# A long convolution, linear attention and two mixtures of experts: mixtures re-ordered, attention's front one batch further ahead

## What is computed

```python
x = x + conv(_layernorm(x))        # long convolution, by DFT
x = x + moe(_layernorm(x))         # mixture of experts
x = x + attention(_layernorm(x))   # causal linear attention, 16 heads of 8
x = x + moe(_layernorm(x))         # the same weights again

def attention(x):                  # q, k, v = split(x @ w_attn)
    q, k = elu(q) + 1, elu(k) + 1
    y[t] = (q[t] . sum_{s<=t} k[s] v[s]^T) / (q[t] . sum_{s<=t} k[s] + 1e-6)
    return y @ w_proj

def moe(x):                        # top-1 of 8 experts, and a shared expert
    logits = x @ gate_w; e = argmax(logits); score = sigmoid(max(logits))
    xs = x * score
    routed = (silu(xs @ rt_gate[e]) * (xs @ rt_up[e])) @ rt_down[e]
    shared = (silu(x @ sh_gate) * (x @ sh_up)) @ sh_down
    return shared + routed
```

## Time and profile before

| | |
|---|---|
| median of 3 runs | 617.75 us (612.2 to 619.62) |
| the profiled execution | 617.06 us |
| its span, first to last instruction | 614.2 us |
| mean granted TensorE clock | 0.924 of full |
| busy in the span: PE, PE weight load | 499.2 us (81%), 384.7 us (63%) |
| busy: DVE, ACT, POOL | 382.8, 249.9, 363.2 us |

### The profile page before, as it was taken

How to read it: one execution, slowest core, us unless ns; L and a number is a source line. 1 busy time by engine, 2 the same in 40 slices (tenths; PEclk the granted TensorE clock), 3 DMA queues, 4 the chain that set the end, 5 groups by cost and what they waited for, 6 DMA issues and landing times.

```text
span 614.2 us, 13049 instructions
## 1 busy us (share of the span) xinstructions
PE 499.2 (81%) x3876; PEld 384.7 (63%) x3876; DVE 382.8 (62%) x1191; ACT 249.9 (41%) x639; POOL 363.2 (59%) x490
## 2 busy tenths in 40 slices
PE   2456999986899799994878878888877999899960
PEld 0244787775666599973555655565646665699950
DVE  3645899877765666633566576666556676666633
ACT  2123353422345255542454545454543444255530
POOL 4022665734887156664777787878594886066650
PEclk9968999997999999997788899898986899999995
DMA  8999999900111123315000000000000111133319
GB/s 245 346 199 193 190 190 185 143 1 1 36 48 40 44 81 89 96 53 138 1 3 1 1 3 2 1 3 2 2 2 17 37 43 45 34 85 93 84 53 268
DMA packets 52384, 47.49 MB, mean 77 GB/s; under 512 B 4154, under 2 KB 48891, under 8 KB 52190
## 3 DMA queue, kind: packets, MB, share of 16 engines
q1 hardware_dynamic: 47184, 35.84, 27.3%
q0 software_dynamic: 4544, 9.35, 4.5%
q10 hardware_dynamic: 590, 1.50, 0.8%
HBM read 17.79 MB, written 28.87 MB: 76 GB/s over the span
## 4 chain that ended last, share of the span: by engine, by line
PE 53%; DVE 17%; POOL 11%; issue 10%; ACT 4%; DMA 2%; SPq 1%; DVEq 0%; POOLq 0%; ACTq 0%
PE bank L731 50%; POOL prod L705 4%; DVE residual L1386 2%; POOL step_rstd L258 2%; DVE prod L1329 2%; POOL normed L691 1%; POOL normed L687 1%; ACT silu_sh L1073 1%; PE bank L805 1%; DVE conv_xv L1470 1%; DMA rows<-routed 1%; DVE stats L246 1%; PE bank L741 1%; DVE conv_xv L1238 1%; DVE scores_odd L1543 1%
## 5 line engine op out<-in xcount | busy, mean ns | idle before, releaser
L624 POOL DMA_INDIRECT routed<-row_out,row_token x78 | 75.1, 963 | 72.9 <-DVE row_token L1367 68.7
L731 PE MATMUL bank<-row_in_t,row_weights 128*128 128x128 f32 x624 | 83.8, 277 | 2.8 <-DVE row_weights L1359 1.5
L731 PEld LDWEIGHTS bank<-row_in_t,row_weights 128*128 128x128 f32 x624 | 75.7, 191 | 4.3 <-ACT row_in_t L1052 2.8
L612 POOL DMA_INDIRECT sorted_rows<-rows,place x64 | 62.8, 982 | 20.5 <-issue 13.7
L731 PE MATMUL bank<-prod,silu_sh 32*128 32x512 f32 x256 | 41.1, 715 | 27.8 <-POOL prod L705 27.8
L1052 ACT ACTIVATE wide<-bank 128x512 f32<-128x512 f32 x56 | 30.8, 597 | 79.3 <-PE bank L741 57.8
L731 PE MATMUL bank<-wide,weights_sb 128*128 128x512 f32 x128 | 58.9, 603 | 0.4 <-ACT row_out L1052 0.4
L705 POOL TENSOR_SCALAR prod<-silu_sh,tables_sb 128x256 f32<-128x256 f32 x64 | 36.4, 585 | 25.2 <-DVE silu_sh L1529 25.2
L731 PE MATMUL bank<-experts,row_act 128*128 x312 | 50.2, 283 | 1.4 <-ACT row_out L1052 0.8
L1359 DVE TENSOR_SCALAR row_weights<-experts 128x512 f32 x78 | 33.6, 430 | 27.1 <-issue 24.4
L1092 ACT ACTIVATE row_silu<-bank 128x256 f32<-128x256 f32 x78 | 30.0, 384 | 48.5 <-PE bank L731 47.9
(11 more groups left out here) (176 smaller groups left out, 1135.2 us busy)
## 6 DMA issues: line engine op xcount, KB each, us to landing
sorted_rows<-zeros SPq DMA_DIRECT2D x1, 17028.0 KB, 98.8
row_in<-sorted_rows SPq DMA_DIRECT2D x78, 64.5 KB, 1.8
rows<-routed SPq DMA_DIRECT2D x16, 256.0 KB, 4.5
out<-residual SPq DMA_DIRECT2D x8, 256.0 KB, 4.0
tables_sb<-tables SPq DMA_DIRECT2D x1, 1536.0 KB, 16.7
routed<-row_out,row_token POOLq DMA_INDIRECT x78, 2.4
experts<-rt_gate SPq DMA_DIRECT2D x1, 1024.0 KB, 10.2
experts<-rt_up SPq DMA_DIRECT2D x1, 1024.0 KB, 12.8
```

The source lines that it names most:

```text
L612: pool.indirect_dma_start(sorted_rows, bass.IndirectOffsetOnAxis(ap=place[:, t:t + 1].bitcast(U32), axis=0), rows[:, t, :], None).then_inc ...
L624: pool.indirect_dma_start(routed, bass.IndirectOffsetOnAxis(ap=row_token[:, r:r + 1].bitcast(U32), axis=0), row_out[:, r, :], None).then_i ...
L731: return pe.matmul(out_, lhsT, rhs, start=start, stop=stop, **kw)
```

## The change

- **Mixtures, order.** In each step PE's `turn` goes behind `up` and `rank`, ACT's `keep` behind the Silus. The first steps that stood whole beside the last steps of the layer before are taken apart into `turn`, `gate`, `rank`, `up_half`, `choose`, `find_place`, `apply_kept` and so on, each placed by itself. The first pair's shared `up` and Silu move there too.
- **Tile table.** `tile_table` is split; its first part (experts) goes ahead of that step's gate-up, the second behind it, `blank_table` into the row tiles' start. Three weight buffers instead of two, the first three filled ahead.
- **Late shared pair.** In both layers, in halves: `up` of the first half stands ahead of the last two row-downs.
- **Final loads.** `routed` is laid out so that a partition's 32 tokens follow each other; in the second layer the readback goes to a contiguous tile (2 KB for a partition and DMA instead of four times 512 B), with a semaphore for each.
- **Attention.** `att_in` and rstd have a lead of 5, transpose, projection, features and v a lead of 4; `qk` and `v_wide` have three buffers. Normalizing moves from POOL to ACT (`att_apply`), for which DVE makes the negated mean times rstd (`att_shift`).

```diff
-BACK_PARTS = ((1, 7), (3, 3, 1, 1))
+BACK_PARTS = ((1, 7), (1,) * 8)
-WEIGHT_BUFS = 2
+WEIGHT_BUFS = 3
-SHARED_LATER = (1, 0)
+SHARED_LATER = (1, 1)
-    c["token_numbers"] = row + P * np.arange(TILES)[None] * 1.0
+    c["token_numbers"] = row * TILES + np.arange(TILES)[None] * 1.0
+        down_banks = (bank[1], bank[2])
+        later_silu_banks, later_up_banks, later_down_bank = (bank[5], bank[2]), (bank[0], bank[3]), bank[1]
-        qk = silu_sh
+        qk_third = sb("qk_third", [P, PT])
+            return (silu_sh[:, 0, :], silu_sh[:, 1, :], qk_third[:])[b % 3]
-        v_wide = sb("v_wide", [P, 2, AT, V_N])
+        v_wide = sb("v_wide", [P, 3, AT, V_N])
+        def results(m, first, n):
+            if m == 0:
+                return rows[:, first:first + n, 0:D]
+            return scores_odd[:].rearrange("p (t d) -> p t d", t=TILES)[:, first:first + n, :]
+        routed_v = routed[0:NO_TOKEN, :].rearrange("(p t) d -> p t d", p=P)
-                sp.dma_start(rows[:, k * PAIR:(k + 1) * PAIR, 0:D],
-                             routed[k * PT:(k + 1) * PT, :].rearrange("(j p) d -> p j d", p=P)
+                sp.dma_start(results(m, k * PAIR, PAIR), routed_v[:, k * PAIR:(k + 1) * PAIR, :]
...
-            pipelined([(2, att_qz), (2, clear_future(0)), (4, att_rstd), (4, att_normed), (3, att_by_head),
-                             (2, clear_future(1)), (0, beside(pair_rstd, {12: (0, 1, 2), 13: (3, 4, 5), 15: (6,)}, 2)),
-                             (0, beside(moe_step, {14: (-3, -2), 15: (-1,)}, 2))], B, 2)
+            pipelined([(2, att_qz), (2, clear_future(0)), (5, att_rstd), (3, att_by_head),
+                             (2, clear_future(1)), (0, beside({11: rstds(0), 12: rstds(1, 2), 13: rstds(3, 4, 5), 14: first_exps, 15: second_exps}, 2))], B, 2)
...
-                one_step([(GATE_AHEAD, gate), (TURN_AHEAD, turn), (0, shared_first(m, up)), (GATE_AHEAD, rank),
+                one_step([(GATE_AHEAD, gate), (0, shared_first(m, up)), (GATE_AHEAD, rank), (TURN_AHEAD, turn),
...
+                def first_half_later():
+                    pe.wait_ge(row_copied, RT * (m + 1))
+                    pe.wait_ge(row_acted, RT * (m + 1) - 3)
+                    up_half(PAIRS - 1, 0)
+                pipelined([(3, each(row_turn)), (2, each(row_up_)), (0, each(row_down_)),
+                           (0, beside({RT - 3: first_half_later}))], RT)
+                pe.wait_ge(row_acted, RT * (m + 1))
+                up_half(PAIRS - 1, 1)
+                down(PAIRS - 1)
...
+            def first_gate():
+                gate(0)
+                turn(1)
+            def beside_last_gating():
+                rank(0)
+                gate(1)
+                turn(2)
+                pe.wait_ge(c_prod, 4 * PAIRS)
+                up_half(0, 0)
             pipelined([(1, each(turn_value)), (2, each(project)), (0, each(inverse)),
-                           (0, beside(moe_step, {7: (-1,)})), (1, each(forward)),
-                           (3, each(conv_turn)), (0, beside(moe_step, {6: (-4,)})), (0, each(project_out)),
-                           (0, beside(moe_step, {6: (-3, -2)}))], PAIRS, 1,
+                           (0, beside({7: beside_last_gating})), (1, each(forward)),
+                           (3, each(conv_turn)), (0, beside({6: first_turn})), (0, each(project_out)),
+                           (0, beside({6: first_gate}))], PAIRS, 1,
                       {-3: filter_start, -2: filter_network, -1: spectrum_first, 6: tables_there})
+            rank(1)
+            gate(2)
+            turn(3)
+            up_half(0, 1)
+            rank(2)
...
+            pipelined([(2, att_scores(0)), (0, beside({15: third_gate}, 2)), (0, att_turn_y),
+                           (0, beside({14: first_gate, 15: third_rank}, 2)),
+                           (4, att_turn), (1, att_values), (0, beside({14: first_rank}, 2)), (0, att_out),
+                           (0, beside({14: second_gate}, 2)),
+                           (4, att_project), (1, att_y_back), (0, beside({14: first_shared}, 2)),
                            (2, att_turn_keys), (2, att_scores(1)),
+                           (2, att_state), (2, att_den), (0, beside({13: first_turn}, 2))], B, 2)
...
+            def att_apply(i, r):
+                b = 2 * i + r
+                act.wait_ge(a_shift, b + 1)
+                wait(act, ln_a.turned, b)
+                for j in range(AT):
+                    act.activation(normed[:, j, :], residual[:, b * AT + j, :], ACT.Identity,
+                                   bias=step_shift[:, j:j + 1], scale=step_rstd[:, j:j + 1]).then_inc(ln_a.normed, 1)
...
+            pipelined([(4, att_apply), (2, att_scores_copy(0)), (0, beside({15: fourth_keep}, 2)), (0, att_yt_copy),
+                            (0, beside({14: second_keep}, 2)), (4, att_normed), (1, att_y_copy),
+                            (4, att_features), (2, att_k), (4, att_v), (2, att_scores_copy(1)),
+                            (0, beside({13: first_keep, 14: third_keep}, 2))], B, 2, {13: silu_table})
...
             def step(n):
+                one_step([(-1, shared_first(m, add_shared))], n)
                 if n == PAIRS - GATE_AHEAD:
+                    tile_experts()
+                one_step([(GATE_AHEAD, choose), (0, shared_first(m, gate_up(0))), (0, shared_first(m, gate_up(1))),
+                          (APPLY_AHEAD, apply_kept), (GATE_AHEAD, find_place)], n)
+                if n == PAIRS - GATE_AHEAD:
+                    tile_bases()
                 if n == PAIRS - GATE_AHEAD + 1:
+                    for tile in range(WEIGHT_BUFS):
+                        row_expert(tile)
...
+            pipelined([(4, att_shift), (1, att_state), (1, att_den), (0, beside({14: first_choice, 15: third_choice}, 2)),
+                            (2, att_mask(0)), (5, att_in), (0, att_add), (0, beside({14: first_place, 15: third_place}, 2)),
+                            (1, att_divide), (0, beside({14: second_choice}, 2)), (4, att_feature_sum), (3, att_k_sum),
+                            (2, att_mask(1)), (0, att_stats),
+                            (0, beside({12: first_applies, 14: second_place}, 2))], B, 2)
```

263 lines of the change are left out of this document (175 added, 88 removed).

## The result

| | before | changed |
|---|---|---|
| median of the runs, us | 616.93 (612.2 to 619.62, four runs) | 589.73 (588.75 to 594.3, four runs) |
| ratio, 95% interval | | 0.9582 (0.9503 to 0.966): faster |
| profiled execution / its span, us | 617.06 / 614.2 | 589.13 / 587.1 |
| mean granted TensorE clock | 0.924 | 0.936 |

The forecast was 593 with a range of 580 to 605; the gain was 27.2 us where 24.8 were worked out. The total came out inside the range. Its parts did not come out as worked out, as this account by stages shows. Each stage ends at the start of an instruction in the two profiled executions; the spans differ by 27.1 us.

What follows compares the result with a forecast made beforehand. It took a chain inside each attention step, ending in TensorE's wait on POOL's `prod`, and the seams between stages to hold what could be gained. Terms summed to 24.8 us off 617.06, 592.3; forecast 593, range 580 to 605.

Steps and rivals of the forecast that it cites:

- The bound of attention: In attention, TensorE's wait on POOL's `prod` ends last; with the front one batch earlier, DVE's mask comes next, 8.9 us.
- The second chain: In attention, stats, `att_shift` and two ACT applies after the mask make TensorE's transpose wait 0.26 us more: step 9.16 us.
- Rival 2: Attention gains nothing, its step held at 9.95 us by an unseen loop (ACT's later score copies): 605 us; chance 0.12.
- The lower clock: In attention, the 5.4 us excess from steps at TensorE's lower clock was left as it is.
- rival 1: In attention the clock stays up, 5.4 us more gained: 587 us; chance 0.17 with what lies below 587.
- The fill: At attention's start, `att_in(2)` and its rstd stand in front of the first POOL products: cost 2.0 us.
- The seam into the first gating: Before the first layer's gating, `inverse(7)` goes ahead of work that waits for DVE: gain 4.0 us, bounds 0 and 6.
- The seam after attention: Into the second layer's gating, first two applies move into attention's step 12: gain 2.0 us, bounds -2 and 6.
- Gating steps: In both layers' gating, `turn` behind `rank` gives the second DVE gate-up time: 0.8 us a layer, 1.6 in all.
- Seams into row tiles: From down(6) to the third row-up: gain 1.3 us in the first layer, 5.6 in the second.
- The tail: At the kernel's end, 2 KB readback packets take 1.3 us off, pair 7's late half adds 0.8: gain 0.5 us.
- rival 4: In attention, ACT's Identity needs two table loads a step beside Exp: 635 us; chance 0.05, shared with another such wait.

Runs made afterwards that it cites:

- attention alone: Attention's front alone moved one batch ahead, with the apply on ACT and shift on DVE, against the kernel before: 596.99 us, ratio 0.9642.

## Why the prediction was right or wrong

**The bound of attention, right.** The wait on `prod` was named as the one that ends last, as a chain inside one step; the lead taken back shows both. What would be late next was named as well: DVE's mask and the bank it frees, 8.83 and 0.1 for the signal. A step is 8.91.

**The second chain, wrong.** The sum put 0.26 us on top, for the transpose that waits for ACT's applies, counting that TensorE is ready for it 1.34 us into the step. The applies do end when it said, 1.55 us into the step, but TensorE comes to that transpose only at 1.68 and waits for nothing. Its scores take 1.47 instead of 1.14, because ACT's third copy of the scores before them is late:

```profile
387.34 1.58 ACT L1155 ACTIVATE wide<-bank 128x512 f32<-128x512 f32 x3 [0.27 <-PE bank L775]
```

It ends at 388.92, when the next scores have begun (388.61), and their last group needs the bank that it frees; in the kernel before the scores began 0.8 us after it. Rival 2 named this copy. The delay does not add to the step in full either: `att_y_back` comes 6.11 us into the step where it came at 5.95, and DVE's scan no longer waits for the sum in front of it. That is 9.16 - 8.91 = 0.25 a step, 3.75 us under the gain.

**The lower clock, wrong, and the main miss.** The excess of 5.4 us was left as it was, and its going was rival 1 (587, nearer to the 589.7 measured than the forecast). Steps of 9.95 us with 8.2 us of TensorE work had five of fifteen at 11.1 to 11.4 before, and two with the lead taken back; at 9.30 with 8.20 of work none of the last thirteen had it, and at 8.91 the clock is 1.00 in the window shown and 0.99 over the stage. That the shorter wait keeps the clock up is read from these rows; no run changes the wait and nothing else. The rule of the Trainium skill ("TensorE: Matmul & The Clock Gate", section "What's actually happening"), that activity lifts the throttle, agrees with these rows. With 15 x 1.04 = 15.6, 5.4 of clock and 2.1 for shorter first and last steps (the last alone, which has no front beside it, took 7.36) the 23.1 are accounted for.

**The fill, right.** 2.0 worked out; 2.28 measured (11.34 to 13.62), of which attention alone has 1.48.

**The seam into the first gating, right in kind, near in size.** `inverse(7)` starts at 144.69, 0.05 after the last spectrum sum, and takes 3.72 instead of 5.88:

```profile
144.69 3.72 PE L775 MATMUL bank<-tables_sb,spect_y 128*128 128x256 f32 x16 [0.75 <-POOL spect_y L686]
```

Up to the second down-projection 3.0 us are gained where 4.0 were worked out for it; the lower clock stands around the first down-projection now. The sum's own working has a slip: 25.27 - 20.2 is 5.1, not 4.9.

**The seam after attention, wrong in sign.** 2.0 was worked out as gain; it is a loss of 3.5. The price of the moved applies was seen (1.7 longer in step 13; 2.56 measured) and the lower bound of -2 allowed for a loss; the loss is larger than that. Not seen was ACT's order: a Silu half that waits for TensorE stands in front of rows for which DVE waits 4.3 us. The 5.7 that its sum starts from has no working in the text. The step of the argument that failed is the analogy, "runs the same way" as the first seam. It was not followed engine by engine on ACT. That the old order takes 43.1 with the fast attention shows that the loss is the order's. How it divides between the applies, ACT's queue and the clock stays open: splitting the applies took 48.56 us, and scaling rows first 44.04 once and 47.40 once.

**Gating steps, under-estimated.** From the second to the seventh down-projection 33.90 became 32.10 in both layers, 1.8 each and not 0.8. The waits for the second gate-up, which the 0.8 stood for, did fall from 1.3 to 0.5 there. The other 1.0 was not in the sum: TensorE's busy time for the same work fell from 32.1 to 31.6, and pauses too short to be listed went.

**Seams into row tiles.** In the second layer 12.04 became 6.49: 5.6, as worked out, with luck, since four of ten kernels with the same order took 8.0 to 8.2 there. In the first, 7.73 became 8.27 instead of 6.4. The clock fell to 0.79 there, which the sum had not, and TensorE was busy for 6.08 us instead of 4.55:

```profile
203.76:212.03 8.27, 6.08 (x38) 5.68 (x38) 4.80 (x14) 1.71 (x5) 0.00 (x0) 0.79 0.20 47
```

In two of the later kernels, at full clock, the same seam took 6.75, near the 6.4.

**The tail.** The delay by the late half was put at 0.8 in each layer; the stores are 1.3 and 1.4 later and 0.8 to 1.1 of that is the half's. That larger packets read faster was right; their gain, 1.3, was not: with 512 B packets back, the end came as soon. The price of the small packets was also read too high. The 270 GB/s of the earlier trace rows is a mean with the end of the transfers in it; the 35 slices of that stretch before the end have a mean of 301:

```profile
GB/s 328 299 348 320 311 324 295 291 287 303 356 299 303 295 283 258 274 348 319 287 287 295 266 270 332 319 299 287 283 295 291 295 299 291 287 160 53 21 20 25
```

The rule of the Trainium skill ("DMA: Bandwidth & Descriptors", section "Specifications"), 512 B as enough for line rate, gives the right time here, 18.54 and 18.48 us; the rates in single slices differ.

**What made the total right** is that an under-estimate of 11.3 in attention met over-estimates of 1.8 and 4.5 at the two seams and 1.2 in the tail, 0.6 more in the fill, and 1.0 in a start that was not in the sum: 9.1 together. That is luck, and with it the forecast was 3.3 us above the measured time.

## What to carry to other kernels

Where a step's bound is a chain of hand-overs inside it, look at a lead before you move work off the engine that ends last; test each alone, since here the move gave nothing without the lead (9.94 us a step, as before). When work of the next stage is slipped into the last steps of a loop, write out the queue of every engine: one instruction that waits (here a Silu) holds up whatever stands behind it, and a seam that won in one place lost in another with the same edit. A shorter wait on TensorE can count for more than its length where the clock stays up with it (5.4 us beside 15.6 here), and its gain may not be seen where the clock is down (44.04 and 47.40 us with the same order); so read the clock of each stretch beside its length before a difference of 2 or 3 us is given to an edit.

## What the runs showed of the hardware

- The same work on TensorE, 299 instructions after attention with the same wait of rank(3), took 36.48 us of busy time at a mean clock of 0.81 and 40.04 at 0.71. The two kernels have the same order on this stretch.
- The place at which TensorE falls to its lower clock differs between kernels that have the same order there: the seam into the second layer's row tiles took 6.49 us at 1.00 in the changed kernel and 8.05 at 0.79 with the 512 B readback.
- In the readback, 2 KB packets moved 280 to 380 GB/s in five slices near its start and 512 B packets 264 to 328, with the same time for reads and writes together (18.48 and 18.54 us from the last store issue to the end).
- ACT's Identity ran beside Exp without a table load (32 applies of 0.49 us, steps of 8.91, and five table loads in the whole kernel, as before), so rival 4 did not come.
- One chip ran each row-tile stage 9 to 11 us longer; of that, TensorE waited 5.4 us in the first layer for ACT's copies of turned rows; in that stage the other profiles list no such wait. The kernel before took 20 to 24 us longer there than in the other groups. Why is not known.
